# A routed expert layer: the first bias of each expert carried through the second layer into one joint bias, its nine products placed elsewhere

## The reference, cut to what matters

```
x_mixed = mix(layernorm(x))                       # three neighbours per token
h       = x_mixed @ W1[p] + b1[p]                 # 512 -> 128, for p = 0..8
paths   = h @ W2[p] + b2[p]                       # 128 -> 512
p*      = argmax(tanh(x_mixed @ Wo1 + bo1) @ Wo2 + bo2)
out     = x + layernorm(layernorm(x) + paths[p*]) * gamma + beta
```

## Time and profile before

| | us |
|---|---|
| median of 3 runs (lowest, highest) | 752.56 (751.38, 755.74) |
| the profiled execution's own time | 751.71 |
| its span, first to last instruction | 749.9 |

### The profile page before, as it was taken

The page is one execution under the profiler, slowest core; times in us unless marked ns, Lnnn a source line. Parts: engine busy times, 40 slices in busy tenths (PEclk is TensorE's granted clock), DMA queues, the critical chain, the costliest instruction groups (busy, mean ns, idle before and its releaser), DMA issues. The chain is left out here.

```text
span 749.9 us, 20567 instructions
## 1 busy us (share of the span) xinstructions
PE 708.2 (94%) x8150; PEld 550.0 (73%) x8150; DVE 375.8 (50%) x993; ACT 339.7 (45%) x743; POOL 197.7 (26%) x281
## 2 busy tenths in 40 slices
PE   4999999999999999999999999998999989788994
PEld 3777787787788778778778778786787777564662
DVE  5455334424424424425334434576568777581675
ACT  3535534535435434444444443543354544541663
POOL 0001001001001001001000011048776775535755
PEclk9999999999999999999999999999999999989997
DMA  8211110110110110110110211251000005348930
GB/s 332 86 56 58 58 50 9 58 56 0 56 56 0 56 56 0 56 56 0 56 56 5 51 56 38 75 136 10 17 15 28 29 31 199 103 164 303 347 137 31
DMA packets 17557, 55.97 MB, mean 75 GB/s; under 512 B 6098, under 2 KB 6354, under 8 KB 14566
## 3 DMA queue, kind: packets, MB, share of 16 engines
q1 hardware_dynamic: 13926, 40.64, 15.9%
q0 software_dynamic: 3584, 14.69, 5.1%
HBM read 46.93 MB, written 10.49 MB: 77 GB/s over the span
## 5 line engine op out<-in xcount | busy, mean ns | idle before, releaser
L96 PE MATMUL pj<-W_both 128*128 128x512 f32 x544 | 222.1, 408 | 10.1 <-DVE W_both L595 10.0
L98 PE MATMUL pj<-W_both 128*128 128x512 f32 x544 | 213.8, 393 | 0.0
L97 PE MATMUL pj<-W_both 128*128 128x512 f32 x544 | 212.7, 391 | 0.0
L96 PEld LDWEIGHTS pj<-W_both 128*128 128x128 f32 x544 | 102.8, 189 | 43.2 <-issue 23.6
L98 PEld LDWEIGHTS pj<-W_both 128*128 128x128 f32 x544 | 102.6, 189 | 23.0
L236 POOL COPY q_b<-Q_T 128x128 f32 (+1 forms) x32 | 9.3, 290 | 416.3 <-PE tp L359 349.3
L97 PEld LDWEIGHTS pj<-W_both 128*128 128x128 f32 x544 | 103.0, 189 | 19.2
L493 ACT ACTIVATE K<-pj,bk 128x512 f32<-128x512 f32 x64 | 44.1, 689 | 136.4 <-PE pj L98 136.4
L654 DVE CUSTOM_DVE_ANT_0 m_flat<-sc,mask 128x257 f32<-128x257 f32 x64 | 24.7, 424 | 116.5 <-PE tp L359 95.2
L508 ACT ACTIVATE p_flat<-m_flat,nmax 128x257 f32<-128x257 f32 x128 | 63.8, 501 | 25.5 <-DVE nmax L654 25.4
L500 ACT ACTIVATE V<-pj 128x512 f32<-128x512 f32 x64 | 38.2, 596 | 73.3 <-PE pj L98 71.8
(11 more groups left out here) (365 smaller groups left out, 1149.7 us busy)
## 6 DMA issues: line engine op xcount, KB each, us to landing
raw<-ctx_dram SPq DMA_DIRECT2D x15, 1024.0 KB, 4.8
experts<-w_dram SPq DMA_DIRECT2D x6, 768.0 KB, 5.8
raw<-w_dram SPq DMA_DIRECT2D x4, 1024.0 KB, 4.9
x_nat<-x_dram SPq DMA_DIRECT2D x2, 1024.0 KB, 12.1
rows<-z3s SPq DMA_DIRECT2D x8, 256.0 KB, 2.0
rows<-x_nat SPq DMA_DIRECT2D x8, 256.0 KB, 3.1
rows<-xm SPq DMA_DIRECT2D x8, 256.0 KB, 2.2
raw<-wk_dram SPq DMA_DIRECT2D x2, 512.0 KB, 5.7
```

The lines of the kernel that those rows point to most:

```text
L96: eng.matmul(out, a_hi, b_hi, start=first, stop=False)
L97: eng.matmul(out, a_lo, b_hi, start=False, stop=False)
L98: return eng.matmul(out, a_hi, b_lo, start=False, stop=last)
```

## The change

The product of `b1` with the second layer, plus `b2`, is computed once for each expert and used as the only bias. `b1` arrives as its own tile, 128 x 9. `spread_b1` (in the place of `split_biases`, after DVE's `body(4)`) lays it out so that nine accumulating products `b1_apart[e] x W2[e]` leave the nine biases in rows 0 to 8, and again in 32 to 40, of one PSUM bank. Two of the nine stand on PE behind `rows_transposes(1)`, seven in the place of `idle(5)`. The new `split_biases` waits for them and splits the sum, behind `list_tokens` on DVE; `outputs(0)` waits for it. `hidden` has no bias product any more. As the products need a bank (the fourth of `pa`), the transposed rows of the tiles alternate between two banks and no longer three. Nine gathers go out before the steady loop of POOL, no longer ten; the tenth is issued in that loop behind the first root. `biases` is 41 x 512, no longer 41 x 640, which shortens the memset at its start. SP issues one DMA for `b1` in the place of two that read it with its two dimensions exchanged.

```diff
@@ tiles @@
-        b1_raw, biases = sb("b1_raw", [KB, P]), sb("biases", [KB, P + D], F32R)
+        b1, b1_apart = sb("b1", [P, E]), sb("b1_apart", [P, E * KB])
+        biases = sb("biases", [KB, D], F32R)
-        AT_ONCE, LANDINGS = 7, 10
+        AT_ONCE, LANDINGS = 7, 9
+        joint_bank = pa[0:KB, 3, :]
         def rows_bank(u):
-            return pa[:, (0, 1, 3)[u % 3], :]
+            return pa[:, u % 2, :]
@@ SyncE @@
-            for name, dst in (("wo2", wo2[:, :]), ("bo1", bo1[:, :])):
+            for name, dst in (("wo2", wo2[:, :]), ("bo1", bo1[:, :]), ("b1", b1[:, :])):
                 eng.dma_start(dst, io[name]).then_inc(ex_in, 16)
             for r in (slice(0, E), slice(32, KB)):
                 eng.dma_start(b2_raw[r, :], io["b2"]).then_inc(ex_in, 16)
-                eng.dma_start(b1_raw[r, :], io["b1"].rearrange("m e -> e m"), allow_slow_non_contiguous=True).then_inc(ex_in, 16)
@@ TensorE @@
             def rows_transposes(u):
-                need(eng, rows_out, u - 2)
+                need(eng, rows_out, u - 1)
-            def idle(n):
+            def joint_biases(es):
                 eng.wait_ge(exw_in, 6 * 16)
-                for _ in range(n):
-                    eng.matmul(pa[:, 2, :], ident[:, :], w1_all[:, 0:D], start=True, stop=True)
+                eng.wait_ge(biases_made, SPREAD)
+                eng.wait_ge(o2lo_made, NT)
+                for e_ in es:
+                    mm = eng.matmul(joint_bank, b1_apart[:, e_ * KB:(e_ + 1) * KB], w2_all[:, e_ * D:(e_ + 1) * D],
+                                    start=e_ == 0, stop=e_ == E - 1)
+                if E - 1 in es:
+                    mm.then_inc(found_pe, 1)
             def hidden(k):
-                eng.matmul(h_bank(k), of_slot[:, k:k + 1].broadcast_to([KB, P]), biases[:, 0:P], start=True, stop=False)
-                                    start=False, stop=c == CT - 1)
+                                    start=c == 0, stop=c == CT - 1)
             def outputs(k):
+                if k == 0:
+                    eng.wait_ge(biases_made, JOINED)
-                eng.matmul(y_bank(k), of_slot[:, k:k + 1].broadcast_to([KB, P]), biases[:, P:P + D], start=True, stop=False)
+                eng.matmul(y_bank(k), of_slot[:, k:k + 1].broadcast_to([KB, P]), biases[:, :], start=True, stop=False)
             rows_transposes(1)
+            joint_biases(range(0, 2))
             positions(1)
...
             slot_lists()
-            idle(5)
+            joint_biases(range(2, E))
@@ VectorE @@
             def split_biases():
-                eng.wait_ge(ex_in, 8 * 16)
-                for r in (hi, lo):
-                    ch3.link(eng.tensor_copy(biases[r, 0:P], b1_raw[r, :]))
-                    ch3.link(eng.tensor_copy(biases[r, P:], b2_raw[r, :]))
-                ch3.link(eng.tensor_tensor(biases[lo, 0:P], b1_raw[lo, :], biases[lo, 0:P].bitcast(F32), ALU.subtract))
-                ch3.link(eng.tensor_tensor(biases[lo, P:], b2_raw[lo, :], biases[lo, P:].bitcast(F32), ALU.subtract))
+                eng.wait_ge(found_pe, SLOTS + 1)
+                ch3.link(eng.tensor_tensor(biases[hi, :], joint_bank[hi, :], b2_raw[hi, :], ALU.add))
+                ch3.link(eng.tensor_tensor(b2_raw[lo, :], joint_bank[lo, :], b2_raw[lo, :], ALU.add))
+                ch3.link(eng.tensor_copy(biases[lo, :], b2_raw[lo, :]))
+                eng.tensor_tensor(biases[lo, :], b2_raw[lo, :], biases[lo, :].bitcast(F32), ALU.subtract).then_inc(biases_made, 1)
+            def spread_b1():
+                eng.wait_ge(ex_in, 7 * 16)
+                ch3.link(eng.memset(b1_apart[:, :], 0.0))
+                ch3.link(eng.tensor_copy(b1_apart[:, 0:(E - 1) * (KB + 1) + 1:KB + 1], b1[:, :]))
+                eng.tensor_copy(b1_apart[:, 32:32 + (E - 1) * (KB + 1) + 1:KB + 1], b1[:, :]).then_inc(biases_made, 1)
                 if it == 4:
-                    split_biases()
+                    spread_b1()
...
             list_tokens()
+            split_biases()
             for k in range(NS - 2):
```

More of the change, by code:

```diff
@@ L930, in self_attention_and_experts @@
         tables, z_stored, xb_made, rows_in = sem("tables"), sem("z_stored"), sem("xb_made"), sem("rows_in")
+        biases_made = sem("biases_made")
         ex_in, exw_in = sem("ex_in"), sem("exw_in")
@@ L945, in self_attention_and_experts @@
         TABLES = 18
+        SPREAD, JOINED = 1, 2
         LIFT = 1.5 * 2.0 ** 23 * P
@@ L2054, in centre @@
                 if k == 0:
-                    eng.wait_ge(ex_in, 9 * 16)
+                    eng.wait_ge(ex_in, 8 * 16)
                 eng.wait_ge(mean_made, k + 1)
```

## The result

| | median | runs | ratio to before | mean granted clock |
|---|---|---|---|---|
| kernel before, first three runs | 752.56 us | 751.38 to 755.74 | | |
| kernel before, six runs | 751.40 us | 750.67 to 755.74 | 1 | |
| changed kernel, six runs | 743.71 us | 741.44 to 744.86 | 0.9886 [0.9859, 0.9912] | 0.987 |
| changed kernel again, other chip | 743.05 us (before: 750.39) | 741.71 to 744.87 | 0.9903 [0.9886, 0.9920] | 0.988 |

Brackets hold the 95% interval. The change makes the kernel 7.3 to 7.7 us faster by the medians, 7.3 to 8.6 by the ratios. The profiled execution of the changed kernel took 741.44 us (span 739.7), its fastest, so the pair of profiles differs by 10.3 us where the medians differ by 7.7.

The account below looks back on a forecast made before the run. PE was taken to bound the slots, busy for all of 47.30 us. 5.6 + 0.75 + 0.1 - 0.1 = 6.35 off the profiled 751.71 gave 745.4, as a median 746.2, rounded to 746.0; range 743.9 to 749.4 us.

Parts of the forecast that it names:

- Slots, 5.6: PE's slots without the first-layer bias product: fourteen by 0.43 us, 0.25 for slot 1, less 0.65, so 5.6 us gained.
- The deduction of 0.65 for register loads: Slots: PE's register loads stay between transposes and first-layer products and may keep 0.09 us a slot, 1.3; half taken.
- The forecast is wrong if PE shows idle time in slots 2 to 15: Sign set for PE's timeline: idle time in those slots would speak against the forecast; no size given.
- DVE's biases in self attention, 0.75: Self attention: six DVE instructions become a memset and two copies, PE's 0.64 us wait for the head norm goes; 0.75 gained.
- Start of the slots, -0.1: Start of the slots: four more records on PE, 1.7 us, delay slot 0's transposes, but cost only 0.1.
- Choices, 0: Choices: the two joint products and two row banks in the place of three fall into slack; 0 taken, 0.3 as bound.
- the memset: Memset of biases at the kernel's start, on DVE's chain: 128 columns fewer, 0.1 us gained.
- Only the visible step: Rival, slots: gaps stay because PE's sequencer makes them, only 0.25 us a slot won; 748.1 us, chance 0.17.
- columns: Rival, slots: a product costs only its columns, 0.12 us for 128, 1.8 in all; 750.0 us, chance 0.07.
- POOL takes over: Rival, slots that scatter and gather: POOL's 3.16 us sets the pace, 2.7 less gain; 748.7 us, chance 0.08.
- The ring: Rival, slots: centre(k) waits for slot k-4's scatter to land, longer landings slow the slots; 755.3 us, chance 0.05.
- Slow clock in the choices: Rival, choices: the two products run at half clock, take 3.4 us, 1.5 reaches the lists; 747.5 us, chance 0.07.

Follow-up runs that it names:

- a5_nine: Changed kernel with all nine joint bias products at the start of the slots and none in the choices: 745.81 us, ratio 0.9925 to the kernel before.
- the pair of zero products: Changed kernel with a product of zeros put back in hidden(k), ahead of the first layer: 749.20 us with 41 rows, 745.42 us with 128.
- a4_six: Changed kernel with six DVE instructions of the old split_biases shapes, results unread, put back in self attention ahead of spread_b1: 745.96 us, ratio 0.9914.
- a6_skip2: Changed kernel without the two joint products in the choices (experts 0 and 1 miss their first bias in the output): 743.11 us, ratio 0.9896.
- a8_noring: Changed kernel with result(k) in the slot's own first third and no wait for scatters, bias product still 41 rows: 743.09 us, ratio 0.9896.
- a3_out128: Changed kernel with the joint bias product in outputs(k) padded with zeros from 41 to 128 rows: 743.32 us, ratio 0.9892.
- a7_pad_noring: Changed kernel with the outputs(k) bias product padded to 128 rows, results in the slot's own first third and no wait for scatters: 741.65 us, ratio 0.9878.
- a9_fours: a7_pad_noring with PE's weight offsets loaded for four slots at once, 8 register loads in the place of 32, bounds checks kept: 742.92 us, ratio 0.9888.
- a11_unchecked: a9_fours without the instructions that check each offset's bounds: 740.08 us, ratio 0.9847.
- b2_fill: Kernel before with products that only fill: two in the choices, seven in the place of five at the start of the slots: 751.57 us, ratio 0.9999.

## Why the prediction was right and where it failed

**Slots, 5.6: right in the cost of the product, by luck in the deduction.** From the start of slot 2's transposes to that of the last outputs' second-layer products it was 739.38 - 689.71 = 49.67 before and 729.14 - 685.12 = 44.02 after: 5.65, where the prediction had 6.0 - 0.65 = 5.35. From slot 1's transposes to slot 2's it was 2.59 and 2.40: 0.19, where it had 0.25. In all 5.85 for 5.6. The 5.65 is 14 x 0.449 less some 0.6. The 0.43 a slot was 0.02 too low. The deduction of 0.65 for register loads came out in size by luck: it was half of 0.17 in each slot, and what happened is that in three slots a load met the issue of a gather. The second profile of the changed kernel has 0.7 us of this, a5_nine none. "The forecast is wrong if PE shows idle time in slots 2 to 15" was met in these three by tenths.

By the Trainium skill (TensorE: Matmul & The Clock Gate, "Step-by-step: what each phase is for") the number of rows of a weight load does not matter. For the load itself the pair of zero products agrees: 0.18 us with 41 rows, 0.19 with 128. What the number of rows changes here is whether loads run ahead of the products, and that is worth 0.449 against 0.113 a slot. The 0.056 us for one product, from which the prediction worked out 0.8 us, is half of the 0.113 measured with equal rows.

**DVE's biases in self attention, 0.75: the step that failed.** The prediction said of the wait that goes "What is late next is PE itself. I take 0.75". The place itself gave 0.84. But PE then reaches the scores at 609.9 that much earlier, and the stall of 0.80 in them does not come: 1.6 us in all. So the term was half of what it had to be, because the gain was taken to end where PE stopped waiting for DVE. That the stall goes with DVE's six instructions is shown by a4_six, which brings it back. The stall stood in the profile of before, marked "issue"; the prediction followed the gain to the end of its own loop step and no further. What makes it is argued only: the queue of instruction transfers moves 16 KB at 609.1 us in the kernel before and none in the changed one between 609.0 and 610.6, where the like transfer runs at 603.4. The same holds for all sixteen profiles: the third transfer of this queue behind 590 us starts at 608.8 to 610.0 in the four with the cut and at 601.9 to 605.6 in the twelve without. In the row below (before, 609.0 to 610.4; packets, MB, share) that transfer is seen:

```profile
q8 instruction: 1, 0.02, 5.4%
```

So PE may have run out of fetched instructions among 128 short products. Against it stands that in the kernel before the transfer has ended at 610.3, and the stall starts at 610.95. No run here moved that transfer by itself, and the cause of the stall stays open.

**Start of the slots, -0.1: right.** Lists to slot 0's transposes: 683.46 - 676.27 = 7.19 before, 680.31 - 671.92 = 8.39 after, 1.2 more where 1.4 was expected. Lists to slot 1's: 687.11 - 676.27 = 10.84 before, 682.72 - 671.92 = 10.80 after. Four more records stand where the gather was waited for.

**Choices, 0: right for the products, as far as can be told.** From the scores at 644 to the lists the profiled pair has 31.9 and 29.4 us, by the shorter slow clock after (3.4 us in the place of 6.8), but that is the luck of one pair. Of the profiles with 6.8 us slow there, the one without the two products has 31.9 and five with them 31.3 to 32.1; with 3.4, 29.3 without and 29.4 to 30.9 with them. With 10.2 us slow, two without the products have 32.4 and one with them 31.6. And the medians of a6_skip2 and the changed kernel agree.

**Sum.** 5.85 + 1.6 + 0.1 (the memset takes 0.48 in the place of 0.59) = 7.6, against 7.3 and 7.7 by the medians. Of the 2.3 us between 746.0 and 743.71, 1.2 are the base: the forecast stood on a median of 752.56 of three runs, which six runs put at 751.40. Some 0.85 are self attention and 0.4 the slots and their start, less the 0.2 by which 746.2 had been rounded. The low end's own terms, taken from 746.0, give 746.0 - 0.65 - 0.14 - 1.2 = 744.0 and not 743.9. A low end that took in the scatter of the base's own median too would have held the time.

**The rivals.** "Only the visible step" and "columns": refuted by the period of 2.917, and by the pair of zero products. "POOL takes over": not at 2.92; it does at 2.53, after seven slots. Its price was slightly off: six slots that keep 3.37 are 6 x 0.43 = 2.6, not 2.7, and with nine gathers out early it is seven slots that scatter and gather. "The ring": DVE did wait for scatters in the changed kernel, at no cost (a8_noring is even). "Slow clock in the choices": not so in the profile; the two products take 1.8 us there (658.87 to 660.71), the full clock's pace.

## What to carry to other kernels

- A product whose operands have fewer rows than its neighbours can cost more than its columns: here, with 41 rows among 128, 0.34 us of 0.45, on both of its sides. Try filling its rows with zeros before the algebra is rearranged around it: by the pair of zero products that alone would have bought 0.34 of the 0.45 us of a slot, an estimate, since it was not run. Look then for what takes it back: the second such product, padded in a3_out128, brought the free period down by 0.36 us and the time not at all.
- When a wait goes, follow the engine that comes earlier to its next "issue" gaps, and put the scatter of the base's own median into the range.
- When a bound is lifted and nothing is won, take away the suspects one by one: the wait that a profile names (the ring) was not the cause, register loads in the sequencer and the checks behind them were.

## What the runs showed of the hardware

- PE's load of a register from SBUF takes 0.30 us, but up to 1.35 when it starts while POOL issues an indirect gather; beside an indirect scatter's issue 0.30 to 0.32 (28 of 28). Not every load beside a gather is slow (12 of 22 were under 0.6), and a few beside neither took up to 0.59, so that the cause is not shown. POOL's small instruction behind the gather grows too (1.14 in the place of 0.60, in a7_pad_noring).
- One load of four values takes 0.33 to 0.34 us, up to 1.08 beside a gather's issue. A slot with such loads and the checks of their bounds was 0.4 to 1.3 us longer (a9_fours), and the first three such slots were at the free pace without the checks (a11_unchecked).
- A product of 41 rows among products of 128 keeps its own weight load and the next from running ahead: 0.449 us a slot against 0.113 with 128 rows, while the load itself takes 0.18 and 0.19.
- With filling products for PE (b2_fill) the mean granted clock was 0.987 in the place of 0.984, and the time the same (0.9999 [0.9983, 1.0016]).
